# A transformer tower on one Trainium2 core: the decision tree of tiles 0 to 47 worked in the drain of the last attention layer, outputs in two row halves with four buffers, and the normalised rows later on VectorE

## The reference

```
h = tok_embedding(x)                         # layernorm with gamma, beta
h = h + attn0(layernorm(h))
h = h + experts(layernorm(h))                # top 2 of 8
h = h + attn1(layernorm(h))                  # scores + relative-position scores, softmax, values
h = h + fff(layernorm(h))                    # the tree

def fff(inputs):                             # depth 11, weights 21 x 192
    logits = inputs @ weights_in.T           # 21 nodes
    idx = 0
    repeat 10 times: idx = clip(2*idx + 1 + (logits[idx] > 0), 0, 20)
    coeff[node] = sum over visited nodes of gelu(logits[node])
    return coeff @ weights_out               # 21 x 192
```

## Time and profile before

| what | us |
|---|---|
| median of three runs | 1744.02 |
| the profiled execution's own time | 1748.81 |
| its span, first to last instruction | 1747.1 |
| layer 1 in the loop's rhythm, window 1225 to 1640 | 415 |
| last residual of the layer on DVE (L746) starts | 1687.2 |
| last instruction of the layer on DVE ends | 1688.5 |
| first turn of coefficients on PE (L1494) starts | 1708.1 |
| first output on DVE (L1560) | 1711.9 |

### The profile page before, as it was taken

One profiled execution on the slowest core, in us unless ns is written; L12 is line 12 of the kernel. 1 busy time (PEld: TensorE's weight loads), 2 busy tenths in 40 slices (PEclk: granted clock), 3 DMA queues, 4 the chain that ended last, 5 costly groups with the idle time before them and its releaser, 6 DMA issues. The chain is left out here.

```text
span 1747.1 us, 59084 instructions
## 1 busy us (share of the span) xinstructions
PE 1589.6 (91%) x18950; PEld 1451.9 (83%) x18950; DVE 1277.0 (73%) x2904; ACT 1125.6 (64%) x3085; POOL 798.5 (46%) x1455
## 2 busy tenths in 40 slices
PE   3999999998379999999999999588999999999856
PEld 2888888887269999999999999487888888888743
DVE  5899999996774555555555554477999999999855
ACT  2899999997273333333333333487999999999821
POOL 4566666763013222323232321555677777767200
PEclk9999999999699999999999999688999999999958
DMA  4122222222117988888889886577788888888704
GB/s 125 44 71 72 69 72 69 73 69 54 51 41 208 260 255 256 257 257 256 257 255 258 256 257 182 134 198 194 212 231 231 220 225 234 225 217 229 199 1 144
DMA packets 350387, 302.16 MB, mean 173 GB/s; under 512 B 44637, under 2 KB 315442, under 8 KB 350322
## 3 DMA queue, kind: packets, MB, share of 16 engines
q1 hardware_dynamic: 329984, 261.37, 53.9%
q0 software_dynamic: 16032, 37.51, 8.1%
q10 hardware_dynamic: 4306, 2.44, 0.6%
HBM read 208.17 MB, written 93.05 MB: 172 GB/s over the span
## 5 line engine op out<-in xcount | busy, mean ns | idle before, releaser
L1075 ACT ACTIVATE prob<-ps_s,b1s 128x256 f32<-128x256 f32 x426 | 179.0, 472 | 345.1 <-PE ps_s L1042 302.6
L1042 PE MATMUL ps_s<-xhi,w1hi_c 128*128 128x256 f32 x852 | 236.8, 296 | 1.6 <-ACT xhi L1068 1.6
L970 POOL DMA_INDIRECT xs<-zn_d,idx x71 | 68.7, 967 | 366.6 <-PE ps_t L1006 364.9
L1042 PE MATMUL ps_s<-xhi,w1lo_c 128*128 128x256 f32 x852 | 227.0, 284 | 0.0
L1017 PE MATMUL ps_v<-probT,prob 128*128 128x192 f32 x852 | 208.3, 326 | 0.0
L1017 PE MATMUL ps_k<-probT,prob 128*128 128x192 f32 x852 | 208.1, 326 | 0.0
L406 PE MATMUL ps_q<-xT,wqk_c 128*128 128x128 f32 x1536 | 205.1, 286 | 2.2 <-ACT xT L638 2.2
L406 PEld LDWEIGHTS ps_q<-xT,wqk_c 128*128 128x128 f32 x1536 | 196.5, 201 | 5.5 <-ACT xT L638 3.1
L617 ACT ACTIVATE kT<-ps_q,halves 128x128 f32<-128x128 f32 (+1 forms) x512 | 173.4, 366 | 4.8
L1042 PEld LDWEIGHTS ps_s<-xhi,w1hi_c 128*128 128x128 f32 x852 | 164.1, 193 | 2.0 <-ACT xhi L1068 2.0
L1042 PEld LDWEIGHTS ps_s<-xhi,w1lo_c 128*128 128x128 f32 x852 | 164.3, 193 | 0.0
(11 more groups left out here) (227 smaller groups left out, 4203.0 us busy)
## 6 DMA issues: line engine op xcount, KB each, us to landing
rel_d<-rpad SPq DMA_DIRECT2D x64, 864.0 KB
relb<-rel_d SPq DMA_DIRECT2D x64, 768.0 KB
probT<-w2h SPq DMA_DIRECT2D x71, 576.0 KB
score<-w1h SPq DMA_DIRECT2D x71, 384.0 KB
score<-w1h SPq DMA_DIRECT2D x142, 192.0 KB
ys_d<-ys SPq DMA_DIRECT2D x71, 192.0 KB
tok<-b2h SPq DMA_DIRECT2D x71, 96.0 KB
posb<-pos_w SPq DMA_DIRECT2D x128, 48.0 KB
```

The source lines that it names most:

```text
L970: pool.indirect_dma_start(xs[b][:, s, :], None, zn_d, bass.IndirectOffsetOnAxis(ap=ix[b][:], axis=0)).then_inc(x_ld[b], 16)
L1042: last = pe.matmul(dst, w, x, start=(k == 0), stop=(k == len(terms) - 1))
L1075: last = act.activation(hT[b][:, c, :], ps_s[:, j, (c % 2) * BLK:(c % 2) * BLK + BLK], ACT.Gelu, bias=b1s[b][:, c:c + 1])
```

## The change

Three things are altered.

1. In DVE's body of layer 1 the call of `normalised_rows` moves from the head to behind `add_relative`.
2. The barrier between the layer and the tree goes. The tree is worked in two parts, tiles 0 to 47 (`early`) and 48 to 63 (`late`). `pipeline` has a hook `behind(n)` that is called after each step written out at the end. DVE works `early` behind steps 68 to 71, ACT its Gelu behind step 69, POOL fills fc and fr with their first values behind 66 and 67. The test "logit > 0" and the product with the parent are one instruction. `late` stands between outputs: before m = 1 and before m = 3.
3. The outputs: no gathering copy (PE turns fc itself), the turned coefficients are used as two halves of 64 rows with 64-row matmuls, ho4 has four buffers, and SP issues the stores in a row.

```diff
-def pipeline(eng, ages, body, links=None, per=0, tiles=NT):
+def pipeline(eng, ages, body, links=None, per=0, tiles=NT, behind=None):
...
     for n in range(head + UNROLL * rounds, tiles + max(ages.values())):
         body(Step(ages, n, n // 2, n % UNROLL, tiles))
+        if behind:
+            behind(n)
...
                 else:
-                    normalised_rows()
                     normalise_sums(0)
                     expert_sum(0)
                     normalise_sums(1)
                     expert_sum(1)
                     add_relative()
+                    normalised_rows()
                     expert_sum(2)
...
+        fg, fr = in_tiles(relb[1], NODES), in_tiles(rpad[0], NODES)
+        prod = in_tiles(relb[0], LEAVES)
+        cT4 = [relb[0][:].rearrange("p h s -> p (h s)")[:, 1024 + 128 * p:1152 + 128 * p] for p in range(2)]
+        ho4 = [score[p // 2][:].rearrange("p g a k -> p (g a k)")[:, 4 * D * (p % 2):4 * D * (p % 2) + 4 * D]
+               .rearrange("p (k d) -> p k d", k=4) for p in range(4)]
+        EARLY = 12
+        PARTS = [slice(0, 4 * EARLY), slice(4 * EARLY, NT)]
+        turn_bank = [ps_k, ps_q]
+        def decode_pool(pool, n):
+            if n == 66:
+                pool.memset(fc[:], 0.0).then_inc(F_["fc"], 1)
+            if n == 67:
+                pool.wait_ge(M[1]["rst"][0], 16 * (NT // 2))
+                pool.memset(fr, 1.0).then_inc(F_["fr"], 1)
+        def decode_turn(pe, m):
+            p = m % 2
+            pe.wait_ge(F_["ready"], 1 if m < EARLY else 2)
+            pe.wait_ge(L[1]["pt_sb"], 3 * NT)
+            after(pe, F_["cT_sb"], m - 1)
+            pe.transpose(turn_bank[p][:, 0:128], fc[:, 4 * m:4 * m + 4, :].rearrange("p k n -> p (k n)"), ident[:])\
+                .then_inc(F_["cT_ps"], 1)
+        def decode_product(pe, m):
+            p = m % 2
+            pe.wait_ge(F_["cT_sb"], m + 1)
+            pe.wait_ge(L[1]["s_rd"], NT)
+            after(pe, F_["o_sb"], m - 1)
+            for side in range(2):
+                r = slice(64 * side, 64 * side + 64)
+                last = pe.matmul(ps_s[:, 2 * p + side, 0:2 * D], cT4[p][r, :],
+                                 wout4[r, 2 * side:2 * side + 2, :].rearrange("p k d -> p (k d)"),
+                                 start=True, stop=True)
+            last.then_inc(F_["o_ps"], 1)
+            def scaled(self):
+                tiles = self.ts.stop
+                self.dve.wait_ge(L[1]["rsz_ok"], tiles)
+                self.dve.wait_ge(L[1]["y_ok"], tiles)
...
+                self.dve.wait_ge(L[1]["s_rd"], NT)
+                self.dve.tensor_tensor(self.fg, self.lg, scale, ALU.mult).then_inc(F_["scaled"], 1)
...
+                    k(self.dve.scalar_tensor_tensor(self.children(fr, lo, n, 1), self.lg[:, :, lo:lo + n], 0.0, parent,
+                                                    ALU.is_gt, ALU.mult))
...
+        def decode_output(dve, m):
+            p, q = m % 2, m % 4
+            dve.wait_ge(F_["o_ps"], m + 1)
+            dve.wait_ge(L[1]["p_sb"], NT)
+            after(dve, out_st[q], 16 * (m // 4))
+            dve.tensor_tensor(ho4[q].rearrange("p (s k) d -> p s k d", s=2),
...
                 pipeline(sp, AGES[1], body)
+                for m in range(NM):
+                    sp.wait_ge(F_["o_sb"], m + 1)
+                    sp.dma_start(ov[:, 4 * m:4 * m + 4, :], ho4[m % 4]).then_inc(out_st[m % 4], 16)
...
+                def behind(n):
+                    if n == 69:
+                        decode_gelu(act, 0)
+                act_steps(act, 1, behind)
+                for m in range(NM):
+                    decode_turned(act, m)
+                    if m == 1:
+                        decode_gelu(act, 1)
...
+                def behind(n):
+                    if n == 68:
+                        early.scaled()
+                        early.reach(LEVELS[0:2])
+                    if n == 69:
+                        early.reach(LEVELS[2:4])
+                    if n == 70:
+                        early.coefficients(LEVELS)
+                    if n == 71:
+                        early.last_reach()
+                        early.leaves()
+                dve_steps(dve, 1, behind)
+                for m in range(NM):
+                    if m == 1:
+                        late.scaled()
+                        late.reach(LEVELS)
+                    if m == 3:
+                        late.coefficients(LEVELS)
+                        late.last_reach()
+                        late.leaves()
+                    decode_output(dve, m)
```

More of the change, by code:

```diff
@@ L313, in tower, with pool_steps @@
         block_a = ctx2.enter_context(nc.Block())
-        def pool_steps(pool, l):
+        def pool_steps(pool, l, behind=None):
             S, M_, ages = L[l], M[l], AGES[l]
@@ L364, in pe_project, with pe_steps @@
             return pe.matmul(dst, x1, w[1][:], start=False, stop=True)
-        def pe_steps(pe, l):
+        def pe_steps(pe, l, behind=None):
             S, ages = L[l], AGES[l]
@@ L545, in body, with act_steps @@
                     scores()
-            pipeline(pe, ages, body)
-        def act_steps(act, l):
+            pipeline(pe, ages, body, behind=behind)
+        def act_steps(act, l, behind=None):
             S, ages = L[l], AGES[l]
@@ L661, in body, with dve_steps @@
                         turned_probs(2)
-            pipeline(act, ages, body)
-        def dve_steps(dve, l):
+            pipeline(act, ages, body, behind=behind)
+        def dve_steps(dve, l, behind=None):
             S, M_, ages = L[l], M[l], AGES[l]
@@ L873, in body @@
                     output_moments()
-            pipeline(dve, ages, body, ch, 9 if l == 0 else 6)
+            pipeline(dve, ages, body, ch, 9 if l == 0 else 6, behind=behind)
         B_ = {n: sem("B_" + n) for n in ("g_ex", "dve", "cnt_ps", "ready", "pool", "placed", "turned_ps", "turned",
@@ new lines, in tower @@
+        F_ = {n: sem("F_" + n) for n in ("fc", "fr", "scaled", "gelu", "dve", "ready", "cT_ps", "cT_sb", "o_ps", "o_sb")}
+        out_st = [sem(f"out_st{p}") for p in range(4)]
+        NM = NT // 4
+        EARLY = 12
[7 more added lines that the diff above has]
+                pool.memset(fr, 1.0).then_inc(F_["fr"], 1)
@@ new lines, in decode_gelu, with decode_turned @@
+        def decode_gelu(act, part):
+            act.wait_ge(F_["scaled"], part + 1)
+            act.activation(fg[:, PARTS[part], :], fg[:, PARTS[part], :], ACT.Gelu).then_inc(F_["gelu"], 1)
+        def decode_turned(act, m):
+            p = m % 2
+            act.wait_ge(F_["cT_ps"], m + 1)
+            after(act, F_["o_ps"], m - 1)
+            act.activation(cT4[p], turn_bank[p][:, 0:128], ACT.Copy).then_inc(F_["cT_sb"], 1)
+        def decode_turn(pe, m):
[5 more added lines that the diff above has]
+                .then_inc(F_["cT_ps"], 1)
@@ L1422, in _ @@
                 pipeline(sp, AGES[1], body)
+                ov = out.rearrange("t b d -> b t d")
+                for m in range(NM):
+                    sp.wait_ge(F_["o_sb"], m + 1)
+                    sp.dma_start(ov[:, 4 * m:4 * m + 4, :], ho4[m % 4]).then_inc(out_st[m % 4], 16)
+                for q in range(4):
+                    sp.wait_ge(out_st[q], 16 * (NM // 4))
             @block.gpsimd
@@ L1447, in _ @@
                 dve.wait_ge(h1_ld, 16 * NT)
[L1448 to L1473, removed]
@@ new lines, in _ @@
+                ch = Chain(dve, F_["dve"])
+                early, late = Decode(dve, ch, 0), Decode(dve, ch, 1)
+                def behind(n):
[9 more added lines that the diff above has]
+                        early.leaves()
```

140 lines of the change are left out of this document (54 added, 86 removed).

## The result

The changed kernel takes 1718.59 us (median of 4 runs, 1716.83 to 1724.36) beside 1744.60 for the kernel before: a ratio of 0.9861, 95% interval 0.9837 to 0.9885, so 26 us or 1.4% faster. Timed again later it gave 0.9865 (0.9832 to 0.9898). The forecast was 1711 in a range of 1700 to 1722; rival A said 1717.

The account below looks back on a forecast made before the run. DVE, with its wait for POOL's rs, was taken to set the loop step, and latency the end. 27.1 us from the tail plus 5.8 from the step gave 32.9: 1711 us from the median 1744.0, range 1700 to 1722.

Parts of the forecast that it names:

- rival A: Loop: the relb round trip replaces the rs wait, step stays 8.235 us, only the tail gains: 1717 us; chance 0.24.
- the ring: Loop: DVE's scores, ACT's Exp and copies, rpad store, relb load, back to DVE; 24.8 us against three steps of 24.7.
- The step: Loop: xn behind relb's addition removes the 0.62 us rs wait; step 8.235 to 8.12, gaining 5.8 us.
- What can give is ACT's wait: Loop: ACT's 0.47 us wait for PE's values can shrink, since on comes about 1 us earlier.
- rival E: Loop: store and load slow each other, 2.8 us more over three steps, 47 us in all: 1764 us; chance 0.03.
- PE's floor: Loop: PE limits the step next, 8.235 less its 0.23 us wait for on: 8.0, plus 0.04 for branches.
- Drain: After the loop: early tree, 10.0 us, mostly hidden; 0.9 us added on ACT's path and 0.5 by the last piece.
- First output: Tail: no barrier, most of the tree in the drain; first output at 1691.0 instead of 1711.94, 20.9 us gained.
- Outputs: Tail: late tree 6.9 us; last twelve outputs at 1.15 to 1.65 us each, 15.8 us, then 2.7 for landing.
- Rival D: Outputs: DMA rate does not rise with four in flight, 1.97 instead of 1.15 us each, 11 us: 1722; chance 0.04.
- Rival B: Outputs: PE paces them because halves do not overlap or clock stays low, 4 us: 1715, both 1723; chance 0.12.
- Rival C: Loop: POOL holds the port shared with DVE, up to 0.4 us on DVE each step: 1715 us; chance 0.04.

Follow-up runs that it names:

- kernel in two parts: Changed kernel with the relative scores' store and load each split into two DMAs of six heads, each store with its own semaphore: 1689.24 us, ratio 0.9701.
- the repeat: The changed kernel timed and profiled once more, unaltered, beside other variants: 1717.53 us, ratio 0.9865 to the kernel before.
- full rows: Changed kernel with output products taking all 128 rows of the turned coefficients instead of two 64-row halves: 1717.85 us, ratio 0.9851.

## Why the prediction was right or wrong

**Bound of the loop before: right, but only half of it.** Forecast: DVE with the wait for rs sets the step of 8.235. The kernel in two parts with xn at the head steps by 8.243, and DVE has that wait and no other. What I had not weighed enough: the ring stood at nearly the same height, some 0.13 us a step below. My sum of 24.8 against three steps of 24.7 could not show that, because it holds in any kernel (the legs take in all waits); the slack between relb's last packet and L705, 0.4 us in three steps, does. xn behind L705 takes 0.3 of it, and the longer store leg more than the rest in the first profile.

**The step: wrong, 5.8 us forecast and 0.8 found over the layer (-4.0 in the loop, +4.6 at its start).** The step that failed is "What can give is ACT's wait", with a step of 8.12. In the first profile ACT's leg gave 0.38 and the store leg took 0.55; in the repeat ACT's leg gave nothing, because a wait for PE's relative scores took the place of the one for its values. The step was 8.336 and 8.271, with 0.75 and 0.70 us of waiting for relb a step. The start of the layer, where I had counted 0 with 2 either way, gives some 3 us: 94.1 to 95.6 in five profiles with xn behind, 98.8 and 97.0 with xn at the head. Rival A named what happened; so did the mechanism of rival E, at a tenth of its price. I also took the legs from one instance (6.15 and 5.01) where their means were 5.75 and 5.48: the sum was right, but it hid that the store leg stretches and shrinks. Both figures varied step by step in the trace of before.

**PE's floor: wrong by 0.12.** I had 8.04 from the wait of L363 on on; in the kernel in two parts, with PE busy all the time, the step is 7.92. I take it that other small waits stood in what I counted as its work; which ones was not tried.

**Drain: -1.1 against -1.4.** Gelu and table load stand on ACT's path as forecast (2.3 us together). The early tree takes 2.3, 1.5, 1.8 and 2.8 us, 8.4 together instead of 10.0; only the last piece stands directly before the last residual. How long the drain takes depends more on when the clock falls: from the last L722 to the last residual I found 20.0 us (full rows, clock 0.89 from 1668 to 1674) to 23.9 (seven profiles; in the changed kernel with 0.50 there). The kernel before had 0.50 all through that stretch, and so had four of those seven: 22.8 against 23.9 is the drain's price at one clock.

**First output: right.** 22.1 us for 22.3; the halves took 1.65 at the lower clock, forecast 1.5.

**Outputs: 7.7 against 6.2.** The late tree costs 5.1 instead of 6.9: eight products take 1.0 together, because they are not linked to each other and overlap. From m = 3 written (1696.2) to the last output written (1710.8) 14.6 us, forecast 15.8; the last landing 4.3, forecast 2.7. With two buffers it takes 3.2, so the stores in flight with it seem to lengthen it; this was not tried by itself. Rival D fails: 278 GB/s at a share of 0.86, against 189 and 0.57 with two buffers.

**Rival B fails** on both counts: the halves overlap, and the clock rose at 1691.6. But PE is named in most of DVE's small waits, at 1.11 us an output and not at 1.6; the DMA ends two, one of 1.74 us. Rival C: POOL's add of one column still ends with DVE's L722 (L327 takes 1613 ns in the mean), L827 is as long as before (412 and 408 ns), so the port costs nothing here.

**The sum** came out near (32.9 for 32.0 between the two profiled executions) partly by luck: 5 us too much in the step, 1.5 too little in the tail, and 2.7 of scatter ahead of the layer. By the medians the gain is 26.0 us, which is rival A's 27; 1718.6 lies within the range of 1700 to 1722, but above the forecast's own 1703 to 1716. The kernel with the tail's change alone, at 0.9836, has all of it.

## What to carry over

Where a wait is taken out of a tight loop, look at every ring that crosses DMAs too, as means over many steps: how long its data have lain ready when they are used is its slack (the sum of its legs is not, since it always makes whole steps). A second ring within 2% takes all the gain, and a DMA leg is no constant but grows when its start moves into another's transfer. Before giving up such a move, cut the latency in series: splitting a store and its load in two, each part with its own semaphore, took the round trip out of the loop's bound at the same bytes, and then the move paid some 18 us. In this tail of stores bound by landing the buffers counted most (9 us), PE's halves little (2 us or less).

## What the hardware showed that I had not expected

- Fewer bytes in packets of 320 bytes bought no DMA time: their share was 0.83 at 182 GB/s instead of 0.85 at 223, and the 512-byte packets beside them went from 27 to 41 ns.
- Two DMAs of six heads instead of one of twelve, at the same packets, let a round trip's first half turn round in 3.15 us instead of 6.2.
- With DVE hardly waiting in the two-part kernel, xn (L732) takes 457 ns in the mean instead of 386, and up to 577. The long ones stand beside POOL's gather of tok (L347), 480 ns in the mean of 37. With xn at the head it stands beside POOL's work on sd and takes 379. Whether POOL is the cause was not tried.
